# A two-layer graph network on one core: who issues the projected table's store, and what the last part centres

## The reference

```python
# layer 0: four projections of each node, the weights by node type
h1, h2, h3, h4 = (node_proj(x, W[k], b[k], node_type) for k in 1..4)
w5e = edge_attr_16 @ W5[edge_type] + b5[edge_type]
num = sum(h3[dst] * (h4[src] + w5e), -1)
score = softmax(num / 4, over an axis of length 1)
x = layernorm(x + h1 + segment_sum(score * (h2[src] + w5e), dst))

# layer 1: a softmax over the edges of each destination
m = relu(x[src] + edge_attr_32 @ We + be) + 1e-7
ez = exp(m - segment_max(m, dst)[dst])
agg = segment_sum(m * ez / segment_sum(ez, dst)[dst], dst)
x = layernorm(x + (x + agg) @ Wm + bm)
```

## Time and profile before

| | us |
|---|---|
| median of three runs | 1854.49 (1852.36 to 1854.88) |
| profiled execution, its own time | 1856.25 |
| its span, first to last instruction | 1854.6 |
| PE busy | 1609.4 (87%) |
| DVE busy | 1605.9 (87%) |
| POOL busy | 1332.7 (72%) |
| ACT busy | 755.1 (41%) |

### The profile page before, as it was taken

How to read it: one execution, slowest core, us unless ns; L and a number is a source line. 1 busy time by engine, 2 the same in 40 slices (tenths; PEclk the granted TensorE clock), 3 DMA queues, 4 the chain that set the end, 5 groups by cost and what they waited for, 6 DMA issues and landing times.

```text
span 1854.6 us, 28443 instructions
## 1 busy us (share of the span) xinstructions
PE 1609.4 (87%) x8677; PEld 1032.4 (56%) x8677; DVE 1605.9 (87%) x3258; ACT 755.1 (41%) x1421; POOL 1332.7 (72%) x1391
## 2 busy tenths in 40 slices
PE   6697999999999999998662599999999999999936
PEld 6544666666666655656451255555555555555525
DVE  6644999999998888888677499999999999999966
ACT  4201333333333322323222166665666656666641
POOL 4777777777777777777774677777777777777733
PEclk9798999999999999999885799999999999999965
DMA  8974666666666565655552166666666666666641
GB/s 285 346 237 124 183 181 177 182 174 182 182 177 170 166 174 169 163 165 163 167 157 71 43 178 180 190 185 183 189 186 186 185 186 180 180 183 189 181 116 43
DMA packets 217026, 322.62 MB, mean 174 GB/s; under 512 B 62193, under 2 KB 124202, under 8 KB 216747
## 3 DMA queue, kind: packets, MB, share of 16 engines
q1 hardware_dynamic: 128360, 147.03, 26.6%
q0 software_dynamic: 44464, 70.93, 18.5%
q10 hardware_dynamic: 44052, 102.85, 14.8%
HBM read 187.39 MB, written 133.22 MB: 173 GB/s over the span
## 4 chain that ended last, share of the span: by engine, by line
POOL 65%; issue 21%; PE 4%; DMA 4%; SPq 2%; DVE 2%; ACT 1%; ACTq 0%; POOLq 0%; DVEq 0%
POOL rows L576 30%; POOL block L566 24%; POOL rows L566 8%; DMA d_inj<-zeros 1%; SPq L447 1%; POOL d_inj L586 1%; POOL typed L596 1%; PE bank L783 1%; DMA ntype_i<-in_node_type 1%; POOL H L614 1%; PE wide L974 0%; SPq L412 0%; PE wide L975 0%; DVE run L1189 0%; PE bank L790 0%
## 5 line engine op out<-in xcount | busy, mean ns | idle before, releaser
L576 POOL DMA_INDIRECT rows<-d_x,idx x588 | 557.4, 948 | 186.6 <-issue 178.9
L566 POOL DMA_INDIRECT block<-d_h,idx x504 | 492.2, 977 | 153.6 <-issue 153.3
L927 PE MATMUL wide<-late,ntype_i 125*128 125x512 bf16 x975 | 220.5, 381 | 49.7 <-DVE ntype_i L1270 49.7
L566 POOL DMA_INDIRECT rows<-d_h,idx x182 | 176.1, 967 | 58.6 <-issue 55.2
L927 PE MATMUL wide<-edge_lists,ntype_i 125*128 125x512 bf16 x936 | 209.9, 379 | 0.0
L828 PE MATMUL wide<-late,typed 125*128 125x512 bf16 (+1 forms) x650 | 193.2, 380 | 18.1 <-DVE late L1132 18.1
L660 ACT ACTIVATE keep_late<-keep 128x512 bf16<-128x512 bf16 x98 | 61.7, 630 | 335.3 <-DVE run L1189 335.3
L927 PEld LDWEIGHTS wide<-late,ntype_i 125*128 125x128 bf16 x975 | 96.2, 99 | 155.8 <-DVE ntype_i L1270 50.1
L828 PE MATMUL wide<-edge_lists,typed 125*128 125x512 bf16 (+1 forms) x600 | 175.4, 375 | 0.5 <-DVE edge_lists L1132 0.5
L938 PE MATMUL wide<-ident,block 128*128 128x128 f32 x784 | 141.2, 305 | 34.3 <-DVE block L1310 26.6
L927 PEld LDWEIGHTS wide<-edge_lists,ntype_i 125*128 125x128 bf16 x936 | 91.9, 98 | 100.1
(11 more groups left out here) (223 smaller groups left out, 3435.2 us busy)
## 6 DMA issues: line engine op xcount, KB each, us to landing
d_run<-block ACTq DMA_DIRECT2D x98, 512.0 KB
d_inj<-zeros SPq DMA_DIRECT2D x28, 896.0 KB
inj<-d_inj SPq DMA_DIRECT2D x98, 256.0 KB
d_run<-stage ACTq DMA_DIRECT2D x98, 256.0 KB
feat<-in_ea16x3T SPq DMA_DIRECT2D x196, 96.0 KB
types<-d_type SPq DMA_DIRECT2D x196, 64.0 KB
keep<-d_keep SPq DMA_DIRECT2D x196, 64.0 KB
keep<-d_pen SPq DMA_DIRECT2D x196, 64.0 KB
```

The costliest lines, as they stand in the source:

```text
L566: pool.indirect_dma_start(out=ring[c % RING][:, j, h, :], out_offset=None, in_=d_h24, in_offset=bass.IndirectOffsetOnAxis(ap=idx[:, c, at: ...
L576: pool.indirect_dma_start(out=rows1[c % RING1][:, j, h, :], out_offset=None, in_=d_x1, in_offset=bass.IndirectOffsetOnAxis(ap=idx[:, c, at ...
L927: ins = pe.matmul(p_hot[s], table[q][:, SPLIT * k:SPLIT * (k + 1), :].rearrange("p b c -> p (b c)"), hot[s][:, k, :], start=(k == 0 and q ...
```

## The change

Six edits are made together.

1. The load of `ntype_i` is issued by ACT, first of its program, and no longer by SP.
2. The two transfers that store `d_h24`, and after them the ten loads of `w5`, `we` and `wm`, are issued by ACT between its two runs of 25 copies.
3. SP issues 11 zeros early, then the lists, 4 more zeros, four loads of pick rows, and 13 zeros; the first loads of edge features and flags come after these. It no longer waits for the table's store.
4. DVE makes `row_i` between the typed features of the first six tiles and those of the others.
5. In the last four steps of stage 1 PE does turn1(c-1) ahead of project1(c+2).
6. In the last part `wm` and x1 are centred once (`wm_mean`, `x1_centred`), so that the product comes out centred. Per group, mean, scale and subtraction are gone; ACT squares straight from PSUM; `base` is made for all 25 tiles ahead of the groups. PE adds `x1_centred`, and waits for the normalised group (`s_x1`) where it waited for the subtraction (`s_square`).

```diff
-ZEROS_EARLY = 8
+ZEROS_EARLY = 11
+ZEROS_NEXT = 15
@@ sync
-            sp.dma_start(ntype_i[:, :], t["node_type"].to_broadcast([C + 1, N_NODES])).then_inc(s_nodes, 16)
...
-            (wait for s_wzero, ten loads of w5, we, wm)
...
-            of_node = d_h24.rearrange("(i p) c -> p i c", i=NT)
-            sp.wait_ge(s_sel, NT)
-            for a, b in ((0, WHOLE), (WHOLE, NP)):
-                sp.dma_start(of_node[a:b], H[a:b, :, C:3 * C]).then_inc(s_h24, 16)
+            for z in range(ZEROS_EARLY, ZEROS_NEXT):
+                sp.dma_start(flat[z], zeros[:, :]).then_inc(s_injzero, 16)
+            sp.wait_ge(s_slots, 48)
+            for u in range(SLOTS):
+                sp.dma_start(slots_of_unit(u), rows_of_unit(u)).then_inc(slots_in[u], 16)
+            for z in range(ZEROS_NEXT, ZEROS):
+                sp.dma_start(flat[z], zeros[:, :]).then_inc(s_injzero, 16)
...
-            sp.wait_ge(s_slots, 48)
-            for u in range(SLOTS):
-                sp.dma_start(slots_of_unit(u), rows_of_unit(u)).then_inc(slots_in[u], 16)
-            sp.wait_ge(s_h24, 32)
-            for z in range(ZEROS_EARLY, ZEROS):
-                sp.dma_start(flat[z], zeros[:, :]).then_inc(s_injzero, 16)
@@ scalar
+            act.dma_start(ntype_i[:, :], t["node_type"].to_broadcast([C + 1, N_NODES])).then_inc(s_nodes, 16)
...
+            of_node = d_h24.rearrange("(i p) c -> p i c", i=NT)
+            act.wait_ge(s_sel, NT)
+            for a, b in ((0, WHOLE), (WHOLE, NP)):
+                act.dma_start(of_node[a:b], H[a:b, :, C:3 * C]).then_inc(s_h24, 16)
+            act.wait_ge(s_wzero, 2)
+            (ten loads of w5, we, wm)
...
-                act.wait_ge(s_square, first + g + 1)
-                act.activation(sq[:, nodes_at(g), :], centred[:, nodes_at(g), :], ACT.Square).then_inc(s_squared, 1)
+                if first:
+                    act.wait_ge(s_y, g + 1)
+                    src = wide[g % 2][0:NP, 0:size(g) * C].rearrange("p (i c) -> p i c", c=C)
+                else:
+                    act.wait_ge(s_square, g + 1)
+                    src = centred[:, at, :]
+                act.activation(sq[:, at, :], src, ACT.Square).then_inc(s_squared, 1)
@@ tensor
+                if c >= CHUNKS - 4:
+                    turn1(*chunk_of(c - 1))
                 if c + 2 < CHUNKS:
                     project1(*chunk_of(c + 2))
-                if c >= 1:
+                if 1 <= c < CHUNKS - 4:
                     turn1(*chunk_of(c - 1))
...
-                    pe.wait_ge(s_square, GROUPS + g - 1)
+                    pe.wait_ge(s_x1, GROUPS + g - 1)
@@ vector
+            typed_features(0, FIRST)
             then(dve.memset(mb_col[:, :], 0.0))
             dve.wait_ge(s_signs, NT - NT_DVE)
             then(dve.tensor_scalar(full_rows[:, NT_DVE:NT], full_rows[:, NT_DVE:NT], -0.5, ROWS / 2, ALU.mult, ALU.add))
             dve.tensor_copy(row_i[0:NP, :], full_rows[:, :]).then_inc(s_row_i, 1)
+            typed_features(FIRST, N_NODES)
...
+            then(dve.tensor_reduce(wm_mean[:, :], wm[:, :], AX.X, ALU.add))
+            then(dve.tensor_scalar(wm_mean[:, :], wm_mean[:, :], 1.0 / C, None, ALU.mult))
+            then(dve.tensor_scalar(wm[:, :], wm[:, :], wm_mean[:, :], None, ALU.subtract))
+            then(dve.tensor_reduce(mean[:, :], x1, AX.X, ALU.add))
+            then(dve.tensor_scalar(mean[:, :], mean[:, :], 1.0 / C, None, ALU.mult))
+            then(dve.tensor_tensor(x1_centred, x1, nodes_of(mean[:, :]), ALU.subtract))
             dve.wait_ge(s_mb, 32)
...
+            then(dve.tensor_tensor(base, channels_of(mm[:, :]), nodes_of(cross[:, :]), ALU.mult))
+            then(dve.tensor_tensor(base, base, x1, ALU.add))
```

More of the change, by code:

```diff
@@ L125, in gnn_program @@
         wm = sb("wm", [C + 1, C])
+        wm_mean = sb("wm_mean", [C + 1, 1])
         late_all = sb("late", [NP, KT * PAIR_EDGES // 2])
@@ L634, in _ @@
                 act.activation(H[:, i, C:3 * C], bank[i % 4][0:NP, 0:2 * C], ACT.Copy).then_inc(s_sel, 1)
+            of_node = d_h24.rearrange("(i p) c -> p i c", i=NT)
[3 more added lines that the diff above has]
+            act.wait_ge(s_wzero, 2)
+            for h in range(2):
+                b = h * C
+                act.dma_start(w5[b:b + T_EDGE * F0, b:b + C], t["W5"].rearrange("t f h -> (t f) h")).then_inc(s_weights, 16)
+                act.dma_start(w5[b + T_EDGE * F0:b + T_EDGE * (F0 + 1), b:b + C], t["b5"]).then_inc(s_weights, 16)
+                act.dma_start(we[b:b + F1, b:b + C], t["We"]).then_inc(s_weights, 16)
+                act.dma_start(we[b + F1:b + F1 + 1, b:b + C], t["be"]).then_inc(s_weights, 16)
+            act.dma_start(wm[0:C, :], t["Wm"]).then_inc(s_weights, 16)
+            act.dma_start(wm[C:C + 1, :], t["bm"]).then_inc(s_weights, 16)
             for i in range(NT):
@@ L973, in _ @@
                     for k in range(a, b):
-                        pe.matmul(wide[g % 2][0:NP, k * C:(k + 1) * C], ident[0:NP, 0:NP], x1[:, BOUNDS[g] + k, :], start=True, stop=True)
+                        pe.matmul(wide[g % 2][0:NP, k * C:(k + 1) * C], ident[0:NP, 0:NP], x1_centred[:, BOUNDS[g] + k, :], start=True, stop=True)
                         ins = pe.matmul(wide[g % 2][0:NP, k * C:(k + 1) * C], featsT[g % 2][n][:, (k - a) * NP:(k - a + 1) * NP], wm[:, :],
@@ L1019, in _, with typed_features @@
             then(dve.tensor_tensor(w24[:, :, :, 0], w24[:, :, :, 0], w24[:, :, :, 1], ALU.subtract))
-            for a, b in ((0, FIRST), (FIRST, N_NODES)):
+            def typed_features(a, b):
                 for k in range(2):
                     dve.scalar_tensor_tensor(x_typed[k][:, a:b], ntype_i[:, a:b], float(k), xT[:, a:b], ALU.is_equal, ALU.mult).then_inc(s_typed, 1)
+            typed_features(0, FIRST)
             then(dve.memset(mb_col[:, :], 0.0))
@@ L1206, in _, with normalise @@
                 work(*chunk_of(CHUNKS - back))
-            def layer_norm(src, g, first):
+            def normalise(src, g, first):
                 at = nodes_at(g)
-                then(dve.tensor_reduce(mean[:, at], src, AX.X, ALU.add))
-                then(dve.tensor_scalar(mean[:, at], mean[:, at], 1.0 / C, None, ALU.mult))
-                dve.tensor_tensor(centred[:, at, :], src, nodes_of(mean[:, at]), ALU.subtract).then_inc(s_square, 1)
                 dve.wait_ge(s_squared, first + g + 1)
@@ L1219, in layer_norm @@
                 then(dve.reciprocal(rstd[:, at], std[:, at]))
-                return dve.tensor_tensor(x1[:, at, :], centred[:, at, :], nodes_of(rstd[:, at]), ALU.mult)
+                return dve.tensor_tensor(x1[:, at, :], src, nodes_of(rstd[:, at]), ALU.mult)
+            def layer_norm(src, g):
+                at = nodes_at(g)
+                then(dve.tensor_reduce(mean[:, at], src, AX.X, ALU.add))
+                then(dve.tensor_scalar(mean[:, at], mean[:, at], 1.0 / C, None, ALU.mult))
+                dve.tensor_tensor(centred[:, at, :], src, nodes_of(mean[:, at]), ALU.subtract).then_inc(s_square, 1)
+                return normalise(centred[:, at, :], g, 0)
             for s in range(2):
@@ L1346, in _ @@
                 then(dve.memset(featm[n][C:C + 1, :], 1.0))
+            then(dve.tensor_tensor(base, channels_of(mm[:, :]), nodes_of(cross[:, :]), ALU.mult))
+            then(dve.tensor_tensor(base, base, x1, ALU.add))
             def features_of(g):
                 at = nodes_at(g)
-                then(dve.tensor_tensor(base[:, at, :], channels_of(mm[:, :], size(g)), nodes_of(cross[:, at]), ALU.mult))
-                then(dve.tensor_tensor(base[:, at, :], base[:, at, :], x1[:, at, :], ALU.add))
                 dve.wait_ge(s_got[g], 3 * 16 * size(g))
@@ L1358, in normalised @@
                 dve.wait_ge(s_y, g + 1)
-                ins = layer_norm(wide[g % 2][0:NP, 0:size(g) * C].rearrange("p (i c) -> p i c", c=C), g, GROUPS)
-                ins.then_inc(s_x1, 1)
+                normalise(wide[g % 2][0:NP, 0:size(g) * C].rearrange("p (i c) -> p i c", c=C), g, GROUPS).then_inc(s_x1, 1)
             for g in range(GROUPS):
```

15 lines of the change are left out of this document (4 added, 11 removed).

## The result

| | before | changed | |
|---|---|---|---|
| median | 1854.68 (4 runs) | 1879.28 (4 runs) | ratio 1.0134, 95% interval 1.0122 to 1.0147 |
| profiled execution / its span | 1856.25 / 1854.6 | 1878.81 / 1877.0 | +22.4 in the span |
| POOL's first gather of the table | 58.48 | 94.49 | +36.0 |
| POOL's first gather of chunk 6 | 151.48 | 184.33 | +32.85 |
| POOL's last gather of stage 1 | 1771.42 | 1803.46 | +32.0 |

The change is slower, as was forecast, but by more than the range allowed. Between chunk 6 and the last gather next to nothing moved (32.85 us there, 32.0 here): the head lost these 32 us and the last part gave back 9.6.

What follows compares the result with a forecast made beforehand. POOL's stream was taken to set the end through most of both stages. Head +16.2 and last part -8.4 made +7.8 us, carried to the 1854.49 median: 1862.5 forecast, own range 1856 to 1870, with rivals A and B 1838 to 1872.

Steps and rivals of the forecast that it cites:

- The zeros' wait of 3.60: POOL, before the head's scatter: the 3.60 us wait for zeros would be absorbed, since the zeros are down earlier.
- turns between the queues: Table's store beside zeros: one table row passes per zeros packet, first gather at 78, scatter +16.2 us.
- Rival A: Table's store: several rows pass per zeros packet, first gather at about 57 or 54, total 1841 us; chance 0.29.
- it lands beside the keys as before: Head: moving the load of node types from SP to ACT leaves its landing beside the keys unchanged.
- the one microsecond of delay: Table's store on ACT: 1 us for the later second half of typed features, with issue at about 40.5.
- 34 rows are left against the last thirteen zeros: End of the store's passage: 34 table rows per DMA engine alternate with zeros, taking 9.9 us.
- upper bound of 90: POOL's first gather of the table: latest start at 90, with all 150 other rows passing against zeros.
- Rival B: ACT between its copies: held by its own issues, adding 9 us to the forecast, 1871; chance 0.14.
- upper bound of 37: ACT between its copies: held 37 us, until the store lands at 77, instead of 13 to 14.
- -8.4 forecast: After POOL's last gather: early turn -2.7, base +1.3, groups -7.0, in sum -8.4 us, between -4 and -11.
- Groups 7.4 us apart: Last part: without DVE's reduction, scale and subtraction, a group takes 7.4 us instead of 8.86.
- the two waits of 2.89 and 3.58 us: DVE's idle time for maxima and crossing sums: covers 4.6 us of centring, cost 0, at worst +1.7.

Runs made afterwards that it cites:

- e14: Kernel before with early row numbers, changed last part, late zeros after pick rows, and the table's store issued by ACT instead of SP between its copies: 1864.0 us.
- e4b: Changed kernel, but SP waits for the table's store to land before issuing the last seventeen zeros: 1852.2 us.
- e3b: Changed kernel with the table's two stores issued by SP again, behind eleven zeros and the lists and ahead of the seventeen other zeros: 1848.7 us.
- e1b_tail: Kernel before with only the changed kernel's last part and early turns: 1846.0 us.
- e2: Changed kernel with the load of node types back on SP's queue behind the keys: 1868.2 us.
- e9: Kernel before with the table's store on ACT, twenty late zeros right after its landing, ahead of first features and pick rows, and the changed last part: 1865.5 us.
- e6b: Changed kernel with every transfer of zeros cut in two, 56 of 448 KB for 28 of 896 KB: 1854.7 us.
- e15: As e9, with the four loads of pick rows ahead of the twenty late zeros instead of behind them: 1845.0 us.
- e1_tail: Same kernel as e1b_tail, run on a chip where the kernel before takes 2277.8 us: among four runs there of 2267.3 to 2284.9 us.

## Why the prediction was wrong in size

**Right: what bounds, and the way.** POOL's stream sets the end from the first gather of the table on; the shift at chunk 6 came out at the last gather (32.85 and 32.0). The zeros' wait of 3.60 was absorbed. The 57.5 us from first gather to scatter were 57.8.

**Right: turns between the queues.** Seen in the packet counts of the changed kernel and of e14, and in the time that came back when the zeros were held or the store put in q1. Rival A is refuted: by it the first gather was due at 57 or earlier, and it came at 94.49.

**Wrong: "it lands beside the keys as before".** The step on the load of node types took its move for free. In a queue of its own it took turns with the keys (60 packets against 56 in the first 6 us): keys at 12.4 and not 6.2, with counts, typed features, projections and the table behind them. The store was issued at 46.6; the sum has 41.5, in which the one microsecond of delay stands twice. Undone alone, the move gives 10 to 11 us. It is my own rule of turns that I did not apply to the load that every engine waits for first. Nor were the row numbers earlier: POOL's first gather by them is at 24.87, not 23.20.

**Wrong: "34 rows are left against the last thirteen zeros".** The sum has the first rows pass at once and all 16 DMA engines alike. From its start at 41.5 to the end of the pick rows at 67.5 it passes 161 of the 195 rows and leaves 34. In the trace, at 72.6 us, as long behind the real start, 711 rows of the table were left, 44 for each engine. The ten rows between fit the beginning: the first row of the table moved at 51.05, 4.4 us after the issue. Then the engines drew apart. With turns of 0.31 us (0.28 for a row of zeros, 0.03 for one of the table) 44 rows take 13.6 us, that is until about 86; the last row moved at 93.6, while other engines had been through with the table since 78. Why they drew apart is not shown. The passage took 47.9 us (94.49 - 46.6) where the sum had 36.5 (78 - 41.5).

Together: 5.1 us from the start and 11.4 from the passage, 94.5 against 78. Of the 11.4, some 4 are the first row's delay and some 7 the slowest engine's, by the estimate above. The size of a turn and the way were right.

The upper bound of 90 for the first gather was broken by 4.5 us, since it assumed that the store starts at 41.5; and the range's end of 1872 stopped even short of what that bound gives (1854.5 + 28 - 8.4 = 1874).

**Rival B: the hold came, the cost did not.** ACT was held 37.7 us, and not 13 to 14. That this is near the upper bound of 37 is luck: the bound lets ACT go when the store lands, but ACT was free at 84.3 and the table's last row moved at 93.6. The hold cost nothing here, because `inj` came 32.6 us later and not 16.2. Where the head is repaired (e4b, e3b) PE is late behind it, with 5.06 and 2.72 us of waiting on POOL.

**Right: the last part.** -8.4 forecast, -9.6 in the profile, -7.5 in the runs of e1b_tail. Term by term in the profile: messages(97) -3.9 (forecast -2.7), from there to the first quotient +1.1 (+1.3), the groups -6.8 (-7.0). Groups 7.4 us apart were 7.5 to 7.9. Making the centred copies was hidden as worked out: of the two waits of 2.89 and 3.58 us, 1.70 is left.

## What to carry to other kernels

A second issuing queue did not make a transfer overtake. Beside a queue deep in long rows, the transfer of many short rows paid one long row for each of its own, and landed later than behind the same transfers in one queue. So give a transfer that everything waits for its place ahead of the bulk in the same queue, or hold the bulk back, and look for the next small load that then ends up behind the bulk. Ask the same of the very first loads: a large one moved to a second queue takes turns with them too. An engine that issued transfers between its own operations was held for 11 to 41 us here; what hangs on its next operation must have that much cover. And when an edit is meant to change the length of a turn, look at whether it also changes when the issuer comes to its next transfers, as half the zeros did.

## What the runs showed of the hardware

- Two queues with work waiting shared the DMA engines by rows, not bytes: 340 to 342 packets with 6.5 KB and 0.5 KB each (changed kernel, 56 to 64 us), 276 to 275 (e14, 54 to 60 us), 56 to 60 with 2.7 KB and 12.5 KB (changed kernel, 0 to 6 us).
- From the issue of the table's store to POOL's first gather of it: 14.4 us from SP's queue in the kernel before, 15.8 from ACT's with the late zeros held (e4b), 47.9 from ACT's beside them. The first row moved 4.1 to 4.6 us after the issue on ACT's queue (changed kernel, e2, e4b, e9, e14), and 2.5 us in e6b.
- The 16 DMA engines did not end a transfer together: in the changed kernel the first was through with the table by 78 us, the last at 93.6.
- ACT was held by two stores and ten small loads for 37.7 us in the changed kernel, 41.2 in e2 and 17.7 in e4b, by the two stores alone for 24.8 in e14 and 14.4 in e15, and by the ten loads alone for 11.0 in e3b.
- A broadcast load to 65 partitions in a second queue doubled the time to landing of the keys, from 6.2 to 12.4 us (5.8 with it back in the first queue, e2).
- One chip ran the kernel before in 2278 us instead of 1854. In e1_tail there DVE, ACT and POOL were as long busy as elsewhere, PE 129 us longer at a granted clock of 0.897 instead of 0.944, and the loops waited on PE and on releasers without a name; a comparison on it could not tell what bounds the kernel elsewhere.
